# Moving the weight and attention-vector loads of a graph kernel out of its first phase

## The chip, the cores and the metric

One core of one Trainium2 chip. The metric is the device time of one execution in microseconds (us); the kernel before takes 2069.59 us, the median of 3 runs.

## The reference, cut to what matters

One block of two graph layers over 3750 nodes and 63750 edges that come sorted by destination, 256 features, 8 relations, 4 heads.

```
h = max(layernorm(x), 0)
feat = einsum('ni,rhid->rnhd', h, conv_weights)      # conv_weights: 8 x 4 x 256 x 64
el, er = sum(feat_src * attn_l[edge_type]), sum(feat_dst * attn_r[edge_type])
alpha = softmax over the edges of a destination of leaky_relu(el + er)
x = x + segment_sum(alpha * feat_src) + h_bias
h = max(layernorm(x), 0)
x = x + (linear layer, 3 rounds of mean over neighbours with two 256 x 256 products and relu, linear layer)(h)
```

## The kernel before

The kernel is a row of phases. Each phase is a `nc.Block()`: inside it every engine has its own list of instructions, ordered by semaphores, and at its end all engines meet before any goes on. So a phase lasts as long as its longest engine. DMAs are issued by SP or ACT, each on a queue of its own; an engine that issues a DMA is held while it does so, and the end of a block waits for the issue, not for the landing (the landing has a semaphore of its own, which the user of the data waits for).

The phases at the start, by the line of their block:

- **L327, loading.** SP loads the four integer lists (`dst` twice, `src`, `edge_type`) into `hT`, three DMAs for each list: 3 x 16384 entries, 114 rows of 128, and a rest of 6 (L332, L334, L336). ACT loads the attention vectors, spread to all 128 partitions, into `side` (L342, two DMAs of 1024 KB) and then the weights into `wbuf` (L346, sixteen DMAs of 128 KB, in rows of 256 bytes). POOL makes iotas and fills pads. DVE converts the lists to f32 (L385) when all of them have landed.
- **L396, `tile_ends()`.** DVE picks the first and last key of each tile of 128 edges, PE turns them into a row, DVE copies the row out of PSUM (L400 to L405). ACT, SP and POOL have nothing to do. The function is called a second time with a flag, inside `sort_edges`, for lists that do not come sorted.
- **L424, checks.** DVE works out with a chain of small instructions whether the lists are sorted and spread as planned (L428 to L452); PE has one matmul.
- **L489 and following.** The sort, which is jumped over here, the tile tables (L625), the windows and the load of `x` (L740), then the layer norm and the attention columns (L889). In the last one DVE and POOL multiply the weights by the attention vectors (L914, L932), after a wait for all 18 transfers on the semaphore `s_at` (`s_at` is used nowhere else).
- Behind them the feature tables and the adjacency table (L1133 on, from about 155 us), the walk over the edges, and three aggregation rounds that PE fills.

Of the kernel before, what the change touches and what calls it, by code (L numbers as in the profile page):

```python
# [34 lines left out]
P = 128  # L35
N, E, F, R, H, D = 3750, 63750, 256, 8, 4, 64
LAYERS = 3
K2 = F // P
# [61 lines left out]
def gnn_kernel(nc, x, src, dst, etype, conv_w, attn_l, attn_r, h_bias, w_in, b_in, w_agg, w_self,  # L100
               b_hid, w_out, b_out, out):
    ctx = ExitStack()
    with ctx:
# [15 lines left out]
        def sem(name):  # L119
            names[name] = names.get(name, 0) + 1  # L120
            s = nc.alloc_semaphore(f"{name}_{names[name]}")
            phase_sems.append(s)
            return s
# [157 lines left out]
        def when(eng, flag):  # L281

            if flag is None:
                return nullcontext()
            return eng.If(eng.value_load(flags_i[0:1, flag:flag + 1], min_val=0, max_val=1) > 0)
# [20 lines left out]
        wc = wbuf[:, :].rearrange("p (k n) -> p k n", k=K2)  # L306
        x_all = work[:, 0:8192].rearrange("p (b f) -> p b f", b=32)

        s_ld, s_xl, s_at = [nc.alloc_semaphore(a) for a in ("vectors_loaded", "all_x_loaded", "weights_in")]
# [15 lines left out]
        attn = [side[:, 2048 * i:2048 * (i + 1)] for i in range(2)]  # L325

        with nc.Block() as block:  # L327
            @block.sync
            def _(sp):
                sp.wait_ge(s_pad, 4)  # L330
                for a, buf in zip((dst, dst, src, etype), raw):
                    sp.dma_start(buf[:, 0:3, :], a[0:3 * P * P].rearrange("(c p j) -> p c j", c=3, p=P)  # L332
                                 ).then_inc(s_rl, 16)
                    sp.dma_start(buf[0:whole, 3, :], a[3 * P * P:E - rest].rearrange("(p j) -> p j", j=P)  # L334
                                 ).then_inc(s_rl, 16)
                    sp.dma_start(buf[whole:whole + 1, 3, 0:rest],  # L336
                                 a[E - rest:E].rearrange("(o j) -> o j", o=1)).then_inc(s_rl, 16)

            @block.scalar
            def _(act):  # L340
                for a, buf in zip((attn_l, attn_r), attn):
                    act.dma_start(buf, a.rearrange("(o r) h d -> o (r h d)", o=1).to_broadcast([P, 2048])  # L342
                                  ).then_inc(s_at, 16)
                for k in range(K2):
                    for r in range(R):
                        act.dma_start(wc[:, k, r * F:(r + 1) * F].rearrange("p (h d) -> p h d", h=H),  # L346
                                      conv_w[r, :, k * P:(k + 1) * P, :].rearrange("h p d -> p h d")
                                      ).then_inc(s_at, 16)

            @block.gpsimd  # L350
            def _(pool):
                pool.iota(io_i[:, 0:P], pattern=[[1, P]], base=0, channel_multiplier=0).then_inc(s_io, 1)
                pool.iota(io_i[:, P:P + 1], pattern=[[1, 1]], base=0, channel_multiplier=1).then_inc(s_io, 1)
                pool.iota(lists_i[:, 0:CQ], pattern=[[1, CQ]], base=0, channel_multiplier=0).then_inc(s_io, 1)
                pool.iota(lists_i[:, CQ:], pattern=[[P, NTW]], base=0, channel_multiplier=0).then_inc(s_io, 1)
                for a, v in zip((key, dstm, srcr, typr), (N - 1, -1, PADSRC, 0)):
                    pool.memset(a[:, CR:CT, :], float(v)).then_inc(s_tail, 1)
                pool.memset(fidx_i[:, CR * P:T + U], 0).then_inc(s_tail, 1)
                pool.memset(col_t[:, CR * P:T], -1.0).then_inc(s_tail, 1)
                pool.memset(code_t[:, CR * P:T], 0.0).then_inc(s_tail, 1)  # L360
                pool.memset(typ_t[:, CR * P:T], 0.0).then_inc(s_tail, 1)
                pool.memset(dstloc[:, CR * P:T], -1.0).then_inc(s_tail, 1)
                at = 0
                for c, end in enumerate(CHUNK_END):
                    pool.memset(thr[0:1, at:end + 1], float(c * CW)).then_inc(s_tail, 1)
                    at = end + 1
                pool.wait_ge(s_tail, 9 + NC)

            @block.vector
            def _(dve):  # L370
                for v, buf in zip((N - 1, -1, PADSRC, 0), raw):
                    dve.memset(buf[:, 3:CR, :], v).then_inc(s_pad, 1)
                dve.memset(ones[:, :], 1.0)
                dve.memset(eps_c[:, :], EPS)
                c = Chain(dve, s_c)
                dve.wait_ge(s_io, 2)
                c.link(dve.tensor_copy(iota_w[:, :], io_i[:, 0:P]))
                c.link(dve.tensor_copy(iota_p[:, :], io_i[:, P:P + 1]))
                c.link(dve.tensor_scalar(ident[:, :], iota_w[:, :], iota_p[:, :], None, ALU.is_equal))
                dve.wait_ge(s_io, 4)  # L380
                c.link(dve.tensor_copy(iota_c[:, :], lists_i[:, 0:CQ]))
                c.link(dve.tensor_copy(win_f[:, :], lists_i[:, CQ:]))
                dve.wait_ge(s_rl, 48 * 4)
                for buf, to in zip(raw, (key, dstm, srcr, typr)):
                    dve.tensor_copy(to[:, 0:CR, :], buf[:, 0:CR, :]).then_inc(s_cv, 1)  # L385
                dve.wait_ge(s_cv, 4)
# [3 lines left out]
        base_r, last_r = stg[0:1, 0:T], stg[0:1, T:2 * T]  # L390
        first_c, last_c = small[:, 36:36 + CT], small[:, 44:44 + CT]

        def tile_ends(flag=None):

            s_fc, s_tp, s_br = sem("ends_picked"), sem("ends_turned"), sem("ends_rowed")
            with nc.Block() as block:  # L396
                @block.vector
                def _(dve):
                    with when(dve, flag):
                        dve.tensor_copy(first_c, key[:, :, 0]).then_inc(s_fc, 1)  # L400
                        dve.tensor_copy(last_c, key[:, :, P - 1]).then_inc(s_fc, 1)
                        dve.wait_ge(s_tp, 1)
                        for i, to in enumerate((base_r, last_r)):
                            dve.tensor_copy(to[:, 0:512], PS[0:1, 2 * i, :]).then_inc(s_br, 1)
                            dve.tensor_copy(to[:, 512:T], PS[0:1, 2 * i + 1, 0:T - 512]).then_inc(s_br, 1)  # L405
                        dve.wait_ge(s_br, 4)
                        dve.sem_inc(passed, 1)

                @block.tensor
                def _(pe):  # L410
                    with when(pe, flag):
                        pe.wait_ge(s_fc, 2)
                        for i, c1 in enumerate((first_c, last_c)):
                            for c in range(CT):
                                mm = pe.transpose(PS[0:1, 2 * i + c // 4, (c % 4) * P:(c % 4 + 1) * P],
                                                  c1[:, c:c + 1], ident[:, :])
                        mm.then_inc(s_tp, 1)

        tile_ends()


        s_k, s_ks = sem("check_steps"), sem("check_sum")
        bad, viol = small[:, 0:4], stg[:, 2048:2048 + CR * (P - 1)].rearrange("p (c j) -> p c j", c=CR)
        with nc.Block() as block:  # L424
# [29 lines left out]
            @block.tensor  # L454
            def _(pe):
                pe.wait_ge(s_k, 2)
                pe.matmul(PS[0:1, 0, 0:1], bad[:, 0:1], ones[:, 0:1], start=True, stop=True).then_inc(s_ks, 1)

# [9 lines left out]
        def sort_edges(flag, key_array, other_array):  # L470
# [127 lines left out]


            tile_ends(flag)  # L600

        end_phase()
# [1687 lines left out]
```

## Time and profile before

| | |
|---|---|
| runs | 2069.22, 2069.59, 2075.5 us |
| profiled execution | 2072.4 us, of which the span from first to last instruction is 2070.6 us |
| mean granted TensorE clock | 0.901 |
| busy | PE 1778.8 us (86%), ACT 1143.4 (55%), DVE 1081.7 (52%), POOL 521.1 (25%) |
| first phase (L327) | 0 to 19.0 us |
| tile ends (L396) | 19.0 to 25.1 us |
| checks (L424) | 25.1 to 31.7 us, the end of DVE's last instruction in it |

An engine's busy time does not count the issuing of DMAs: ACT is shown as idle in the first phase although its queue instructions fill it. The queue of an engine has a name of its own in the views, SPq or ACTq.

### The profile page before, as it was taken

The numbers are of one execution on the slowest core, as the hardware profiler recorded it, in microseconds if no ns is written. First come the engines' busy times: TensorE is split into PE (matmuls) and PEld (weight loads), VectorE is DVE, ScalarE is ACT, GpSimd is POOL, SyncE is SP. The second block draws the span as 40 slices with busy tenths as digits, with TensorE's granted clock in tenths as the row PEclk, the third lists the DMA queues.
The fourth block names the chain that finished last, engine by engine and source line by source line (L and its number), as shares of the span: only waits on it lengthen the run. The fifth ranks groups of instructions, "written<-read, shape, count | busy, mean of one in ns | idle before, by whom it ended". The sixth has DMA issues, their size and how long they took to land. (4 is left out here: it accounts for less than half of the span.)

```text
span 2070.6 us, 26209 instructions
## 1 busy us (share of the span) xinstructions
PE 1778.8 (86%) x7604; PEld 1236.5 (60%) x7605; DVE 1081.7 (52%) x3126; ACT 1143.4 (55%) x2498; POOL 521.1 (25%) x544
## 2 busy tenths in 40 slices
PE   1159999999497879798797955999989999999998
PEld 1054444444375557565575634777777777877777
DVE  4858888888365676766767535453550000301011
ACT  0034455565387779797787734454545444544442
POOL 2600000000577777777777300000000000000000
PEclk7569999999687789797898887999999999999999
DMA  4314555555655566565665325333324333363432
GB/s 129 82 14 152 171 195 192 181 201 199 202 146 161 152 182 176 153 188 159 171 173 161 101 63 181 99 123 107 110 77 128 113 116 112 98 208 123 135 123 62
DMA packets 285221, 290.67 MB, mean 140 GB/s; under 512 B 88673, under 2 KB 248102, under 8 KB 284806
## 3 DMA queue, kind: packets, MB, share of 16 engines
q1 hardware_dynamic: 235094, 186.23, 29.3%
q0 software_dynamic: 23952, 66.46, 12.1%
q10 hardware_dynamic: 26016, 36.15, 4.8%
q8 instruction: 64, 1.05, 0.2%
q14 instruction: 95, 0.78, 0.1%
HBM read 201.26 MB, written 87.48 MB: 139 GB/s over the span
## 5 line engine op out<-in xcount | busy, mean ns | idle before, releaser
L1141 POOL DMA_INDIRECT work<-feat_tab,fidx_i x499 | 477.6, 957 | 586.0 <-issue 581.2
L2117 PE MATMUL PS<-a_pe,y_hi 128*128 128x512 f32 (+2 forms) x1440 | 556.7, 392 | 33.4 <-ACT a_pe L2014 33.4
L2117 PE MATMUL PS<-a_pe,y_lo 128*128 128x512 f32 (+2 forms) x1440 | 536.7, 379 | 0.0
L2014 ACT ACTIVATE a_pe<-a_in 128x1536 fp32r<-128x1536 f16 (+1 forms) x240 | 329.3, 1376 | 342.7 <-PE PS L2117 329.1
L2117 PEld LDWEIGHTS PS<-a_pe,y_hi 128*128 128x128 f32 (+1 forms) x1440 | 274.0, 190 | 103.1 <-ACT a_pe L2014 35.0
L1210 ACT ACTIVATE work<-work 128x64 f32<-128x64 f32 x1344 | 325.1, 332 | 0.0
L2117 PEld LDWEIGHTS PS<-a_pe,y_lo 128*128 128x128 f32 (+1 forms) x1440 | 274.2, 190 | 55.2 <-issue 6.7
L1385 PE MATMUL PS<-work,stg 128*128 128x260 f32 x1008 | 289.6, 437 | 6.5 <-ACT work L1210 4.6
L1385 PEld LDWEIGHTS PS<-work,stg 128*128 128x128 f32 x1008 | 207.5, 217 | 65.0 <-issue 19.6
L255 DVE TENSOR_SCALAR side<-iota_c,work 128x512 f16<-128x512 f16 x705 | 245.8, 349 | 0.0
L1325 PE MATMUL PS<-wbuf,hT 128*128 128x512 f32 x480 | 226.9, 595 | 0.0
L2221 DVE TENSOR_TENSOR mean<-PS,rdeg 128x1024 f32<-128x1024 f32 (+1 forms) x24 | 27.2, 1135 | 363.3 <-PE PS L2117 363.0
L273 ACT ACTIVATE side<-PS 128x512 f16<-128x512 f32 x235 | 128.7, 595 | 142.0 <-PE PS L265 69.6
L254 DVE TENSOR_SCALAR side<-iota_c,rel 128x128 f16<-128x128 f16 x705 | 176.9, 251 | 49.1 <-PE PS L265 48.3
L265 PE MATMUL PS<-side 128*128 128x512 f16 x705 | 173.6, 381 | 24.6 <-DVE side L255 16.1
L265 PEld LDWEIGHTS PS<-side 128*128 128x128 f16 x705 | 68.3, 98 | 151.2 <-DVE side L255 36.1
L1335 PE MATMUL PS<-er_win,stg 128*128 128x32 f32 x1008 | 134.9, 294 | 22.5 <-ACT stg L1196 22.5
L1335 PEld LDWEIGHTS PS<-er_win,stg 128*128 128x128 f32 x1008 | 129.9, 211 | 26.4 <-ACT stg L1196 24.5
L1325 PEld LDWEIGHTS PS<-wbuf,hT 128*128 128x128 f32 x480 | 91.8, 191 | 75.1 <-issue 57.9
L1181 ACT ACTIVATE stg<-PS 128x512 f32<-128x512 f32 x120 | 72.0, 600 | 43.3 <-PE PS L1325 42.5
L1588 DVE TENSOR_TENSOR work<-work,PS 128x1024 f32<-128x1024 f32 x42 | 51.3, 1221 | 69.1 <-ACT work L1202 69.1
L1579 DVE TENSOR_TENSOR stg<-PS,dstloc 128x512 f32<-128x512 f32 x126 | 86.4, 686 | 1.5
(257 smaller groups left out, 1674.0 us busy)
## 6 DMA issues: line engine op xcount, KB each, us to landing
a_in<-a_tab SPq DMA_DIRECT2D x210, 384.0 KB, 3.2
feat_tab<-stg ACTq DMA_DIRECT2D x120, 260.0 KB, 2.2
a_tab<-side SPq DMA_DIRECT2D x235, 128.0 KB, 1.8
stg<-dst_tab SPq DMA_DIRECT2D x42, 384.0 KB, 4.0
work<-feat_tab,fidx_i POOLq DMA_INDIRECT x499
h_tab<-outs SPq DMA_DIRECT2D x42, 130.0 KB, 2.6
h_tab<-outs SPq DMA_DIRECT2D x8, 520.0 KB, 3.9
stg<-h_tab SPq DMA_DIRECT2D x8, 520.0 KB, 4.1
```

The source lines that it names most:

```text
L254: dve.tensor_scalar(code[:, s, :], iota_c[:, 0:P], rel[:, k, j:j + 1], None, ALU.is_equal)
L255: dve.tensor_scalar(other[:, s, :], iota_c[:, :], pairs_in[:, w, j, 1:2], None, ALU.is_equal).then_inc(built.pair, 1)
L265: pe.matmul(PS[:, BBS[w % len(BBS)], :], code[:, s, :], other[:, s, :], start=(j == 0), stop=(j == DEPTH - 1)).then_inc(built.free, 1)
L273: act.activation(counts[:, w % KEPT_W, :], PS[:, BBS[w % len(BBS)], :], ACT.Copy).then_inc(built.evicted, 1)
L1141: pool.indirect_dma_start(out=ring[:, s, 0:FE], out_offset=None, in_=feat_tab[:, :], in_offset=bass.IndirectOffsetOnAxis(ap=idx, axis=0)). ...
L1210: ins = act.activation(a, a, ACT.Copy, scale=ring[:, s, F + h:F + h + 1])
L1325: mm = pe.matmul(PS[:, cc, :], hT[:, k, b * P:(b + 1) * P], wc[:, k, cc * 512:(cc + 1) * 512], start=(k == 0), stop=(k == K2 - 1))
L1335: mm = pe.matmul(PS[:, ERB, u * RH:(u + 1) * RH], onehotT[:, u * P:(u + 1) * P], er_win[:, :], start=True, stop=True)
L1385: mm = pe.matmul(PS[:, OUTS[j], 0:EXT], onehot[:, t, :], ring[:, j * U + t, 0:EXT], start=(t == 0), stop=(t == U - 1), skip_group_check=True)
L1579: dve.tensor_tensor(onehot[:, q * QT:(q + 1) * QT, :], IOTA_PS.unsqueeze(1).to_broadcast([P, QT, P]), dstloc[:, tiles_of(i, j, q, QT)].uns ...
L2014: act.activation(a_pe[:, load % A_PE, :, 0:n], a_in[:, load % A_IN, :, 0:n], ACT.Copy).then_inc(s_conv, 1)
L2117: mm = pe.matmul(SUMS(ug, n)[:, f, :], y[0:rows_of, kb, f * P:(f + 1) * P], a_pe[0:rows_of, load % A_PE, kb % KB, 0:n], start=(kb == 0 and ...
```

## The change

The last lines of the diff below stand in the block of the checks (L424). The sixteen weight loads leave the first phase. They are issued in the first call of `tile_ends()`, eight by ACT (the first half of the input features, k = 0) and eight by SP (k = 1). The two loads of the attention vectors are issued by ACT in the phase of checks. In the first phase ACT has nothing left. The semaphore, its count and its waits stay as they are.

```
             @block.scalar
-            def _(act):
-                for a, buf in zip((attn_l, attn_r), attn):
-                    act.dma_start(buf, a.rearrange("(o r) h d -> o (r h d)", o=1).to_broadcast([P, 2048])
-                                  ).then_inc(s_at, 16)
-                for k in range(K2):
-                    for r in range(R):
-                        act.dma_start(wc[:, k, r * F:(r + 1) * F].rearrange("p (h d) -> p h d", h=H),
-                                      conv_w[r, :, k * P:(k + 1) * P, :].rearrange("h p d -> p h d")
-                                      ).then_inc(s_at, 16)
-
...
+        def load_weights(eng, k):
+            for r in range(R):
+                eng.dma_start(wc[:, k, r * F:(r + 1) * F].rearrange("p (h d) -> p h d", h=H),
+                              conv_w[r, :, k * P:(k + 1) * P, :].rearrange("h p d -> p h d")).then_inc(s_at, 16)
+
+        def load_attention(eng):
+            for a, buf in zip((attn_l, attn_r), attn):
+                eng.dma_start(buf, a.rearrange("(o r) h d -> o (r h d)", o=1).to_broadcast([P, 2048])).then_inc(s_at, 16)
+
         def tile_ends(flag=None):
...
             with nc.Block() as block:
+                if flag is None:
+                    @block.scalar
+                    def _(act):
+                        load_weights(act, 0)
+
+                    @block.sync
+                    def _(sp):
+                        load_weights(sp, 1)
...
+            @block.scalar
+            def _(act):
+                load_attention(act)
```

The instructions of ACT from the start of the program to the tile tables, of the kernel before (`UNCONDITIONAL_BRANCH` rows enter and leave a phase):

```order
L2280 ISA
L339 UNCONDITIONAL_BRANCH
L342 DMA side<-in_L_gnn_attn_l 128x2048
L342 DMA side<-in_L_gnn_attn_r 128x2048
L346 DMA wbuf<-in_L_gnn_conv_weights 128x4x64 x16
L327 UNCONDITIONAL_BRANCH
L713 UNCONDITIONAL_BRANCH
```

And of the changed kernel, the same stretch:

```order
L2291 ISA
L396 UNCONDITIONAL_BRANCH
L384 DMA wbuf<-in_L_gnn_conv_weights 128x4x64 x8
L394 UNCONDITIONAL_BRANCH
L466 UNCONDITIONAL_BRANCH
L389 DMA side<-in_L_gnn_attn_l 128x2048
L389 DMA side<-in_L_gnn_attn_r 128x2048
L431 UNCONDITIONAL_BRANCH
```

The loads are split over two phases, weights first, and eight of the weight loads are gone from ACT.

SP of the kernel before, from its last list to the sort:

```order
L332 DMA hT<-in_edge_type 128x3x128
L334 DMA hT<-in_edge_type 114x128
L336 DMA hT<-in_edge_type 1x6
L327 UNCONDITIONAL_BRANCH
L490 UNCONDITIONAL_BRANCH
```

And of the changed kernel, with eight weight loads between the first phase and the sort:

```order
L336 DMA hT<-in_edge_type 1x6
L327 UNCONDITIONAL_BRANCH
L400 UNCONDITIONAL_BRANCH
L384 DMA wbuf<-in_L_gnn_conv_weights 128x4x64 x8
L394 UNCONDITIONAL_BRANCH
L501 UNCONDITIONAL_BRANCH
```

SP's twelve loads of the lists keep their order and stand ahead of every weight load.

## Rows read from the trace of the kernel before

**Rows 1.** The page's chain that ended last, by engine: shares of the span.

```profile
PE 37%; DMA 1%; DVE 1%; ACT 0%; issue 0%; SPq 0%; ACTq 0%; DVEq 0%
```

**Rows 2.** Timeline from 0, DVE: start, duration, what [idle before, released by].

```profile
15.70 1.43 DVE L385 CAST hT<-hT 128x512 f32<-128x512 int32 x4 [12.14 <-DMA hT<-in_edge_type]
19.02 0.17 DVE L400 COPY small<-hT 128x7 f32<-128x7 f32 x1 [1.89 <-PEq L327]
...
24.17 0.53 DVE L405 COPY stg<-PS 1x384 f32<-1x384 f32 x1
25.14 0.69 DVE L428 TENSOR_TENSOR stg<-hT 128x508 f32<-128x508 f32 x1 [0.43 <-PEq L396]
...
31.53 0.14 DVE L452 TENSOR_SCALAR flags_i<-small 1x1 int32<-1x1 f32 x1
```

**Rows 3.** Timeline from 0, queue instructions of ACT: start, duration.

```profile
0.74 0.39 ACTq L342 DMA_DIRECT2D side<-in_L_gnn_attn_l  x1
1.16 0.45 ACTq L342 DMA_DIRECT2D side<-in_L_gnn_attn_r  x1
1.64 16.92 ACTq L346 DMA_DIRECT2D wbuf<-in_L_gnn_conv_weights  x16
```

**Rows 4.** Timeline from 0, queue instructions of SP.

```profile
1.45 0.46 SPq L332 DMA_DIRECT2D hT<-in_dst  x1
1.96 0.41 SPq L334 DMA_DIRECT2D hT<-in_dst  x1
...
3.41 0.61 SPq L334 DMA_DIRECT2D hT<-in_dst  x1
4.06 1.10 SPq L336 DMA_DIRECT2D hT<-in_dst  x1
...
6.18 1.80 SPq L336 DMA_DIRECT2D hT<-in_src  x1
...
8.99 1.01 SPq L336 DMA_DIRECT2D hT<-in_edge_type  x1
```

**Rows 5.** DMA view, 0 to 20 us: busy tenths in 40 slices; queues: packets, MB, share.

```profile
DMA  0005999989897979999999999999999889999999
q10 hardware_dynamic: 8409, 4.12, 79.3%
q1 hardware_dynamic: 2088, 1.02, 21.7%
```

**Rows 6.** DMA view, 16 to 18 us: the queue of ACT (q10).

```profile
q10 hardware_dynamic: 1825, 0.45, 104.3%
```

**Rows 7.** DMA view, 18 to 22 us: ACT's queue and the weight loads' landing.

```profile
q10 hardware_dynamic: 2182, 0.54, 72.2%
wbuf<-in_L_gnn_conv_weights ACTq DMA_DIRECT2D x2, 128.0 KB, 3.2
```

**Rows 8.** Line L346: issue durations in ns, and landing.

```profile
L346 ACTq DMA_DIRECT2D wbuf<-in_L_gnn_conv_weights x16: 456/808/2867, 1.6 to 18.0; - x16
DMA to landing us min/median/max: 3.1/4.8/9.5
```

**Rows 9.** DMA view, 0 to 150 us: a small load: KB each, median us to landing.

```profile
work<-pair_tab SPq DMA_DIRECT2D x78, 3.0 KB, 1.6
```

**Rows 10.** Timeline, later stretches: the next transfer, and the users of the weights.

```profile
43.72 0.42 SPq L703 DMA_DIRECT2D mask_tab<-stg  x1
...
83.22 4.49 POOL L932 TENSOR_TENSOR stg<-wbuf,side 128x2048 f32<-128x2048 f32 x1 [10.26 <-POOLq L740]
83.23 6.63 DVE L914 TENSOR_TENSOR stg<-wbuf,side 128x2048 f32<-128x2048 f32 x1 [3.25 <-PEq L740]
```

**Rows 11.** Stretches: us, busy of PE, PEld, DVE, ACT, POOL, PEclk, DMA share, GB/s.

```profile
200.00:400.00 200.00, 191.75 (x631) 84.24 (x630) 168.14 (x766) 104.82 (x250) 0.00 (x0) 1.00 0.56 182
600.00:1200.00 600.00, 511.39 (x2419) 366.98 (x2418) 402.23 (x1126) 474.00 (x1539) 426.77 (x446) 0.83 0.57 160
```

More of the change, by code:

```diff
@@ L337, in _ @@
                                  a[E - rest:E].rearrange("(o j) -> o j", o=1)).then_inc(s_rl, 16)
-            @block.scalar
-            def _(act):
-                for a, buf in zip((attn_l, attn_r), attn):
-                    act.dma_start(buf, a.rearrange("(o r) h d -> o (r h d)", o=1).to_broadcast([P, 2048])
-                                  ).then_inc(s_at, 16)
-                for k in range(K2):
-                    for r in range(R):
-                        act.dma_start(wc[:, k, r * F:(r + 1) * F].rearrange("p (h d) -> p h d", h=H),
-                                      conv_w[r, :, k * P:(k + 1) * P, :].rearrange("h p d -> p h d")
-                                      ).then_inc(s_at, 16)
             @block.gpsimd
```

## The prediction

> **What bounds the kernel now.** I read the page's chain first. It holds only the end: PE fills the aggregation rounds, and the start of the program doesn't appear in it [rows 1]. The change touches nothing there, so the question is only when the later work begins. Since all engines meet at the end of each phase, a phase that ends earlier by some microseconds should move all that follows by as much. I therefore read the timeline of the first phases, engine by engine, for what each phase ends with.
>
> In the first phase DVE waits until 15.70 us for the last of the integer lists and then converts for 1.43 us, to 17.13 [rows 2]. ACT is later still: its sixteen weight issues fill 1.64 to 18.56 [rows 3]. DVE goes on at 19.02, released by the end of the phase. So ACT's issuing ends the phase, and DVE's wait for the lists stands 1.43 us behind it.
>
> Why the lists are late is in the queue instructions and the DMA view. SP's first issues follow each other by (3.41 - 1.45) / 4 = 0.49 us, but from 4.06 on some of them take 1.01 to 1.80 us [rows 4]. All DMA engines are nearly always busy from 1.5 us to 20 us, and of the 5.14 MB that they move 4.12 MB are ACT's (q10) and only 1.02 MB the lists (q1) [rows 5]. The lists share the engines with transfers that nobody needs before 83 us [rows 10].
>
> **The first phase without ACT's loads.** SP keeps its twelve issues. At 0.49 us each the last begins at 1.45 + 11 x 0.49 = 6.84 us. When has it landed? The nearest small load, from SP and onto idle engines, lands 1.6 us after its issue [rows 9], which gives 8.4. A weight load with others of its queue ahead of it lands after 3.1 at best [rows 8], which gives 9.9. The lists' packets took 21.7% of 16 engines over 20 us for 2088 packets, or 33 ns each, beside the others [rows 5]; spread evenly that is 130 x 33 ns = 4.3 us per engine, less than the 5.4 us over which the issues are spread, so little can pile up. I take 8.8 us, near the lower end.
>
> The Trainium skill has a rule that is a little less kind (DMA: Bandwidth & Descriptors, "Why a DMA increments its semaphore by 16 and not by 1"): a transfer runs on the largest number of engines up to 16 that divides its slowest dimension. By it the 114-row loads use six engines only, and these have 24 + 19 packets per list, 172 in all, which at 33 ns is 5.7 us; begun at about 2.5 us, one us behind the first issue, they end at 8.2 and the wake-up comes some 0.6 us later. By the even spread and the lower bound the landing would be at 8.4 and the next phase 8.7 us earlier; by this rule the landing can't be before 8.8, and it is 8.3. No row here shows which engine takes which packet.
>
> Behind the landing DVE's 1.43 us of conversions stay, and from DVE's last instruction of a phase to its first of the next it is 25.14 - 24.70 = 0.44 us [rows 2]. The next phase then begins at 8.8 + 1.43 + 0.44 = 10.7 us in place of 19.02: **8.3 us earlier**. The bounds, 8.4 and 9.9 for the landing, make it 8.7 and 7.2.
>
> **The phase of the tile ends with sixteen weight issues in it.** DVE and PE need 24.70 - 19.02 = 5.7 us there [rows 2], and ACT and SP have been idle; that is the cover. A weight issue into a queue with room costs 0.46 us at least [rows 8], and with the gap between two issues (1.16 - 0.74 - 0.39 = 0.03 [rows 3]) eight would take about 4 us: hidden. What can spoil it is that the queues fill. 16.92 / 16 = 1.06 us was the mean issue when the engines were full [rows 3], and eight of those are 8.5 us, 2.8 us more than the cover. So the bounds are 0 and 2.8 us.
>
> Which is nearer depends on how many loads a queue takes before it holds its engine. The engines move weights at 0.45 MB in 2 us [rows 6], so one load of 0.131 MB each 0.58 us. From 18.0 us on 0.54 MB are still to be moved [rows 7]; by the end of the last issue at 18.56 some 0.13 MB of these have gone, and 0.41 MB, three loads, are in the queue, without that issue having been slow. With three loads in each of the two queues, ten must have been drained when the last issue is through: 10 x 0.58 us and one us until the first packet (0.74 to some 1.8 in [rows 3, 5]) are 6.8 us, 1.1 more than the cover. With four in each queue it is 8 x 0.58 + 1 = 5.6 us, and nothing shows. I estimate four, as ACT's first issues went in next to two 1 MB loads, and put **0.3 us** of loss.
>
> **The phase of the checks.** ACT's two issues of attention vectors took 0.39 and 0.45 us [rows 3]. They may have to wait for the weights to drain: sixteen loads are through 1 + 16 x 0.58 = 10.3 us after the tile ends began, some 4.3 us into the checks. DVE's chain lasts 31.67 - 25.14 = 6.5 us, so they are covered with 2 us to spare; if that cover were gone, a load of 1024 KB would hold the phase for its own issue only, under a microsecond. DVE and PE of this phase touch neither tile.
>
> **Who waits for the moved loads.** Weights are through at 10.7 + 10.3 = 21 us. The attention vectors are 2 MB in large packets; ACT's queue moved its 4.12 MB in about 19 us beside all else, so 2 MB are through in less than 9.5 us, at 30 us at the latest. The next other transfer is issued at 43.72 - 8 = 36 us, and the users start at 83.2 - 8 = 75 us [rows 10]. Moving the loads costs their users nothing, with 45 us in hand.
>
> **The sum.** -8.3 + 0.3 + 0 = -8.0 us. The profiled execution took 2072.4 us, so its like would take 2064.4; it is 2.8 us above the median of the runs. Against the median: 2069.6 - 8.0 = **2061.6 us**. That is 0.39%; 0.3%, about what a measurement of this kernel can tell from no change, is 6.2 us.
>
> **Rivals.**
>
> - *The queues fill in the tile-ends phase, and ACT or SP ends it.* For it: in the trace nearly all of ACT's weight issues are above the 0.46 us of the shortest (median 0.81, longest 2.87 [rows 8]), and both queues now push at once into engines that drain one load in 0.58 us. Against it: the queues start empty. It costs up to 2.8 us: a gain of 5.5, 2064.1 us, within 0.3%. Two us of it decide. Chance 14%.
> - *The lists are slow by themselves.* For it: the slow issues are always the third of a list, the load of 6 entries, and no row shows that issue without ACT's traffic but the first. If the three slow ones (1.10, 1.80, 1.01 [rows 4]) stay so, the last issue begins at 8.99 as before and lands at 10.6, 1.8 us behind my 8.8: a gain of 6.2, 2063.4 us. Chance 8%.
> - *Slower, by TensorE's clock.* From 200 to 400 us the granted clock is 1.00, the full 2.4 GHz; from 600 to 1200 us the mean is 0.83, so for a third of it, about 204 us, it is at 1.2 GHz, with PE busy 511 of 600 us [rows 11]. PE's work there is cut by waits for gathered rows, and the level changes with them. A shifted start could let more of it fall on the low level. A microsecond at the low level costs half a microsecond at most; to turn 8 us gained into 6.2 lost needs 14.2 us, or 28 us more at the low level, 232 in place of 204. The runs of before differ by 6.3 us with nothing changed, less than half of that. Chance 4%, at 2076 us. The Trainium skill (TensorE: Matmul & The Clock Gate, Part 1) says that the monitor behind this clock runs freely and isn't reset when the kernel starts; by it a shift of 8 us draws new places for the changes but no more of them, which no run so far shows.
> - *The gain is given back, or the loads' place does nothing.* It would take a wait on something that doesn't move with the phases. I found none: every later DMA is issued behind the end of a phase. The same clock can eat 3 to 6 us, though. Chance 9%, 2064 to 2069 us.
>
> **How the numbers follow.** The forecast has 65%: 2060.3 to 2063 us from the bounds of the landing (8.7 and 7.2) and a loss of 0 to 1.1, with some tenths for the clock. The low end of the range is 2059.6. Upwards it takes in the filling queues and the slow lists and part of the give-back, to 2066.5. Faster by over 0.3% (below 2063.4): the forecast but for a small part, and half of the slow lists: 0.66. Within 0.3%: filling queues, the rest of the slow lists, the give-back: 0.30. Slower: 0.04.
>
> **What would show it.** In the profile after: the conversions of the lists begin between 8.4 and 9.9 us; no queue instruction of SP in the first phase is longer than 0.6 us; the first copy of the tile ends at about 10.7 us and the first check at about 17.1, when the last issue of ACT and SP is through; the first checks have two attention issues beside them that end before them; the product of weights and attention vectors begins at 75.2 us and waits for no DMA. I am wrong if the first phase ends later than 12.5 us, if the tile-ends phase lasts over 8 us, or if the 8 us are there at 75 us and gone at the end, which the mean clock of the later stretches would show.

## The result and the profile after

| | before | changed |
|---|---|---|
| median | 2070.32 us (9 runs, 2063.84 to 2078.3) | 2061.33 us (9 runs, 2056.71 to 2071.22) |
| profiled execution, span | 2072.4, 2070.6 us | 2056.7, 2054.9 us |
| mean granted TensorE clock | 0.901 | 0.916 |

The ratio is 0.9955, 95% interval 0.9934 to 0.9975: 0.45% faster, 9 us between the medians. 2061.6 us and 8.0 us had been forecast. (The kernel before has nine runs here, three of them those of the table ahead.)

The timeline of the changed kernel's start, DVE and the two queues (start, duration, what [idle before, released by]), answering to [rows 2 to 4]:

```profile
1.45 0.46 SPq L332 DMA_DIRECT2D hT<-in_dst  x1
...
3.58 0.28 SPq L336 DMA_DIRECT2D hT<-in_dst  x1
...
5.93 0.28 SPq L336 DMA_DIRECT2D hT<-in_edge_type  x1
...
8.93 1.43 DVE L374 CAST hT<-hT 128x512 f32<-128x512 int32 x4 [5.37 <-DMA hT<-in_edge_type]
10.86 5.37 SPq L384 DMA_DIRECT2D wbuf<-in_L_gnn_conv_weights  x8
10.86 5.89 ACTq L384 DMA_DIRECT2D wbuf<-in_L_gnn_conv_weights  x8
10.89 0.17 DVE L407 COPY small<-hT 128x7 f32<-128x7 f32 x1 [0.53 <-PEq L327]
...
16.05 0.53 DVE L412 COPY stg<-PS 1x384 f32<-1x384 f32 x1
17.18 0.55 ACTq L389 DMA_DIRECT2D side<-in_L_gnn_attn_l  x1
17.22 0.69 DVE L435 TENSOR_TENSOR stg<-hT 128x508 f32<-128x508 f32 x1 [0.64 <-PEq L394]
17.75 0.49 ACTq L389 DMA_DIRECT2D side<-in_L_gnn_attn_r  x1
...
23.62 0.14 DVE L459 TENSOR_SCALAR flags_i<-small 1x1 int32<-1x1 f32 x1
28.44 0.69 DVE L641 SCALAR_TENSOR_TENSOR hT<-hT 128x512 f32<-128x512 f32 x1 [4.68 <-PEq L394]
```

The reader is to see four things. The conversions begin at 8.93 in place of 15.70 us, and they, no longer ACT, end the first phase: the first copy of the tile ends stands at 10.89 in place of 19.02, 8.1 us earlier. In the tile ends ACT is through with its issues at 10.86 + 5.89 = 16.75 us, a little behind DVE's last copy at 16.58, and the idle time at the end of the phase has grown from 0.43 to 0.64 us: the cover of 5.7 us was too short by 0.2 us. The attention issues end at 18.2, far inside the checks. And the first instruction of the tile tables stands at 28.44 us, where it stood at 36.36: 7.9 us of shift.

The product of weights and attention vectors, answering to [rows 10]:

```profile
74.89 4.49 POOL L943 TENSOR_TENSOR stg<-wbuf,side 128x2048 f32<-128x2048 f32 x1 [9.84 <-POOLq L751]
74.91 6.63 DVE L925 TENSOR_TENSOR stg<-wbuf,side 128x2048 f32<-128x2048 f32 x1 [2.83 <-PEq L751]
```

83.23 - 74.91 = 8.3 us, and it is the end of a phase that releases both, no DMA. (0.4 us of the 8.3 arise between the tile tables and the product. This stretch takes 46.9 us in the three profiles with the loads in the first phase and 46.4 to 47.0 in the others, so these 0.4 us are within its scatter.) The last packet of the weights ends at 21.8 us and that of the attention vectors at 27.9, where 21 and "30 at the latest" had been forecast. The moved loads cost their users nothing.

The two profiled executions differ by 2070.6 - 2054.9 = 15.7 us, twice that. The last matmul of the feature table (L1325, now L1336) begins at 527.8 us before and 519.5 after, still 8.3 us apart; the last one of the walk over the edges (L1385, now L1396) at 1201.3 and 1185.1, 16.2 us apart:

```profile
L1336 PE MATMUL PS<-wbuf,hT x480: 592/592/1057, 151.9 to 519.5; 128*128 128x512 f32 x160
```

```profile
L1396 PE MATMUL PS<-work,stg x1008: 382/383/800, 565.8 to 1185.1; 128*128 128x260 f32 x168
```

(min/median/max of the duration in ns, first and last start in us.) So this pair gained another 7.9 us inside the walk. There the granted clock was 0.85 in place of 0.83 [rows 11]:

```profile
600.00:1200.00 600.00, 502.61 (x2408) 358.47 (x2407) 410.05 (x1137) 471.95 (x1530) 419.91 (x439) 0.85 0.56 160
```

Over the nine runs of the changed kernel the clock and the time go together: 0.916 has 2056.71 us and 0.898 has 2071.22, with a correlation of -0.78. The spread between executions is 14.5 us wide here, and the profiled execution happens to be the fastest of the nine, so I count these 7.9 us as spread. That the clock causes them isn't shown: in the 27 runs of the kernel before beside e5 to e8 it has a correlation of -0.07 with the time. Nor does the clock explain the gain: its mean is 0.907 over those 27 runs and 0.904 to 0.907 over the runs of each of e5 to e8, which are 9 to 11 us faster.

### The profile page after: what moved, and what is told of

Read it like the earlier page. It is cut to its first block and busy times, and to the rows that moved or that the text cites. A ratio compares the mean times of both kernels' runs of the same rounds, so it can differ in the third digit from the quotient of the medians.

```text
span 2054.9 us, 26209 instructions
## 1 busy us (share of the span) xinstructions
PE 1770.4 (86%) x7604; PEld 1230.3 (60%) x7605; DVE 1081.3 (53%) x3126; ACT 1143.4 (56%) x2498; POOL 520.6 (25%) x544
## 3 DMA queue, kind: packets, MB, share of 16 engines
q8 instruction: 64, 1.05, 0.2%
## 5 line engine op out<-in xcount | busy, mean ns | idle before, releaser
L1396 PE MATMUL PS<-work,stg 128*128 128x260 f32 x1008 | 288.3, 435 | 8.0 <-ACT work L1221 6.2
L1396 PEld LDWEIGHTS PS<-work,stg 128*128 128x128 f32 x1008 | 205.6, 215 | 65.7 <-issue 16.0
L1336 PE MATMUL PS<-wbuf,hT 128*128 128x512 f32 x480 | 226.1, 593 | 0.0
L1336 PEld LDWEIGHTS PS<-wbuf,hT 128*128 128x128 f32 x480 | 91.6, 191 | 74.9 <-issue 57.7
```

Of the source, the lines that this page charges most:

```text
L1336: mm = pe.matmul(PS[:, cc, :], hT[:, k, b * P:(b + 1) * P], wc[:, k, cc * 512:(cc + 1) * 512], start=(k == 0), stop=(k == K2 - 1))
L1396: mm = pe.matmul(PS[:, OUTS[j], 0:EXT], onehot[:, t, :], ring[:, j * U + t, 0:EXT], start=(t == 0), stop=(t == U - 1), skip_group_check=True)
```

## The experiments

Twelve runs, ten of them new kernels and two of them repeats (e8, e12). The early marks are the measure: in each profile the start of the conversions, of the first copy of the tile ends, of the first check, and of the product of weights and vectors. The ratio is to the kernel before, run on the same chip in between. It goes by all the runs of both and isn't the quotient of the two medians beside it. e9 and e10 leave out edges, ran once and have no ratio.

| kernel | conversions | first copy | first check | product | kernel before, this (median us) | ratio (95%) |
|---|---|---|---|---|---|---|
| before | 15.70 | 19.02 | 25.14 | 83.2 | | |
| changed | 8.93 | 10.89 | 17.22 | 74.9 | 2070.32, 2061.33 | 0.9955 (0.9934 to 0.9975) |
| e1_act_waits | 8.97 | 23.04 | 29.16 | 87.2 | 2277.98, 2281.86 | 1.0023 (1.0010 to 1.0035) |
| e2_attention_stays | 12.36 | 14.32 | 20.80 | 78.6 | 2277.98, 2271.47 | 0.9961 (0.9945 to 0.9976) |
| e3_one_queue | 9.03 | 10.99 | 20.23 | 78.3 | 2277.98, 2269.31 | 0.9969 (0.9953 to 0.9986) |
| e4_start_put_back | 19.16 | 21.12 | 27.24 | 84.7 | 2277.98, 2276.08 | 0.9991 (0.9977 to 1.0005) |
| e5_lists_two_queues | 8.49 | 10.45 | 16.88 | 75.0 | 2074.84, 2064.49 | 0.9958 (0.9937 to 0.9978) |
| e6_lists_all_engines | 8.62 | 10.59 | 17.18 | 75.3 | 2074.84, 2065.57 | 0.9947 (0.9926 to 0.9967) |
| e7_weights_in_checks | 8.85 | 10.81 | 16.93 | 75.5 | 2074.84, 2064.98 | 0.9939 (0.9921 to 0.9957) |
| e8_change_again | 9.20 | 11.16 | 17.42 | 75.1 | 2074.84, 2064.18 | 0.9946 (0.9925 to 0.9967) |
| e9_even_lists_only | 8.11 | 10.07 | 16.62 | | | |
| e10_uneven_lists | 8.19 | 10.15 | 16.76 | | | |
| e11_single_loads_last | 8.58 | 10.54 | 16.98 | 75.2 | 2073.20, 2064.56 | 0.9962 (0.9942 to 0.9983) |
| e12_before_again | 16.14 | 19.25 | 25.37 | 83.5 | 2257.31, 2255.16 | 0.9998 (0.9984 to 1.0013) |

In two of the groups, e1 to e4 and e12, every kernel took about 200 us more, all of it in the walk over the edges (in e12, the kernel before itself, its last matmul begins at 1379.5 us and not at 1201.3; the last of the feature table at 527.3 and not at 527.8). They are compared only with the kernel before beside them. The chip isn't the reason: e1 to e4 and e5 to e8 ran on the same one, beside a kernel before of 2278 and of 2075 us.

**e1: the kernel before, ACT waits for the lists.**

```
             def _(act):
+                act.wait_ge(s_rl, 48 * 4)
                 for a, buf in zip((attn_l, attn_r), attn):
```

> The kernel before, with one wait added: ACT begins its eighteen loads in the first phase only when all lists have landed. It tells the two halves of the gain apart, the lists' contention and ACT's issuing. My theory: both are needed, since ACT's issues alone end the phase. The lists then land at about 8.9 us as in the changed kernel, the conversions begin there, but ACT issues from 8.9 on: 2 x 0.45 + 16 x 0.56 = 9.9 us, and the first copy of the tile ends begins at about 19.2 us, as in the kernel before (19.02). Median within 2 us of the kernel before. Rival, the lists' contention is all that counts: the first copy at about 11 us, and 8 us faster.

The conversions begin at 8.97 us as in the changed kernel, and nothing is won: the first copy begins at 23.04, 4.0 us later than before. ACT's queue:

```profile
8.90 0.39 ACTq L343 DMA_DIRECT2D side<-in_L_gnn_attn_l  x1
9.33 0.45 ACTq L343 DMA_DIRECT2D side<-in_L_gnn_attn_r  x1
9.80 12.78 ACTq L347 DMA_DIRECT2D wbuf<-in_L_gnn_conv_weights  x16
```

The theory holds and its size was off: the sixteen issues take 12.78 us, 0.80 each, not 0.56, and the median is 3.9 us above the kernel before, not within 2. The excess is in the third to the fifth weight issue (1.40, 0.99 and 2.64 us): ACT is held there while the attention vectors move, whose last packet ends at 15.8 us. From then on an issue takes 0.53 to 0.56 us again, but for the last (0.72). Both halves are needed: loads that leave the lists alone gain nothing as long as ACT issues them in the same phase.

**e2: the attention vectors stay in the first phase.** The block of the checks loses its two loads, and the first phase gets them back:

```
+            @block.scalar
+            def _(act):
+                for a, buf in zip((attn_l, attn_r), attn):
+                    act.dma_start(buf, a.rearrange("(o r) h d -> o (r h d)", o=1).to_broadcast([P, 2048])
+                                  ).then_inc(s_at, 16)
```

> The changed kernel, with the two attention loads (2 MB, large packets) left to ACT in the first phase. My theory, the engines of the DMA are shared between the queues: the lists (1 MB) wait for part of the 2 MB, which take about 6 us alone; they land at 10 to 12 us in place of 8.9, and the first copy of the tile ends begins at 12 to 14 us: a gain of 5 to 7 us over the kernel before in place of 8. Rival, only the weights with their small packets held the lists up: conversions at 8.9 us as in the changed kernel, first copy at 10.9.

Two megabytes in large packets beside the lists cost them 3.4 us (12.36 in place of 8.93). The theory holds, with sizes a little over its ranges: 12.36 where 10 to 12 was expected, a first copy at 14.32 where it was 12 to 14, and 4.7 us gained at the product in place of 5 to 7. Two of SP's issues show the hold as in the kernel before; these rows and the next two blocks are timelines of SP and DVE:

```profile
3.61 1.39 SPq L336 DMA_DIRECT2D hT<-in_dst  x1
...
5.91 1.85 SPq L336 DMA_DIRECT2D hT<-in_src  x1
```

The weights with their small packets and the attention vectors each take a share of the 6.8 us that the lists were late; about half is the attention vectors'.

**e3: all sixteen weight loads on ACT.**

```
                         load_weights(act, 0)
-
-                    @block.sync
-                    def _(sp):
-                        load_weights(sp, 1)
+                        load_weights(act, 1)
```

> The changed kernel, with all sixteen weight loads on ACT in the phase of the tile ends, none on SP. My theory: sixteen issues at 0.56 us are 8.9 us or more, so ACT ends the phase at 10.9 + 9 = 19.8 and the first check begins at about 20.2 us in place of 17.2: 3 us slower than the changed kernel, 5 us faster than before. Rival, the engines drain at the same pace whatever the queue and the queue holds most of it: first check at 17.2 to 17.5 us, no difference from the changed kernel.

```profile
16.15 0.54 DVE L409 COPY stg<-PS 1x384 f32<-1x384 f32 x1
20.23 0.69 DVE L432 TENSOR_TENSOR stg<-hT 128x508 f32<-128x508 f32 x1 [3.55 <-PEq L394]
```

DVE has done its part at 16.69 and stands idle for 3.55 us until ACT is through: sixteen issues in 8.81 us, 0.55 each. That is the forecast of this experiment to the tenth, and what the split over two engines saves: 3 us. The Trainium skill (DMA: Bandwidth & Descriptors, "Issuing engines are not separate DMA queues") says that issuing from several engines saves only the sequencer's time for the issue, "usually small relative to the DMA itself". The trace agrees on what is saved: the last packet of the weights ends at 21.85 us with one queue and at 21.76 with two. But here, where a phase ends with the issues and not with the landings, the issue time is all that counts.

None of the sixteen issues is longer than 0.53 us: the engines drain a load in about 0.6 us, as the prediction had it, and one queue alone doesn't fill. With two queues it does. The DMA view of the changed kernel from 10.8 to 16.75 us, where ACT's eighth issue ends:

```profile
q1 hardware_dynamic: 2302, 0.57, 50.8%
q10 hardware_dynamic: 2107, 0.52, 48.0%
```

ACT has issued eight loads (1.05 MB) and 0.52 MB have been moved: four loads stand in its queue. ACT's first long issue (0.79 us, at 13.60) and SP's (1.05 us, at 14.04) begin with five and six loads issued and 1.2 and 2.1 moved, so with about four in the queue as well.

**e4: the start put back.**

```
                 dve.wait_ge(s_rl, 48 * 4)
+                for _ in range(11):
+                    c.link(dve.memset(work[:, 0:768], 0.0))
```

> The changed kernel, with eleven clears of an unused stretch of memory (about 0.75 us each, 8.2 us together) on DVE behind the wait for the lists, so that the first phase ends at about 19 us again while all loads stay where the change put them. My theory, the whole gain is the earlier start: time of the kernel before, 2070 us, within 3 us. Rival, a part of the gain comes from elsewhere (the 15.7 us between the two profiled executions against 8.3 us at the start): it stays faster than before, at 2062 to 2065 us.

The clears took 0.93 us each with the wait between them, so the first copy begins at 21.12 and the product at 84.7 us, 1.4 us later than in the kernel before. The gain is gone: 0.9991, an interval that holds 1. It is the earlier start that makes the change faster. By the marks it should have been 1.4 us slower, and its median is 1.9 us lower; more on that below.

**e5: the lists on two queues.** ACT is idle in the first phase; it takes two of the four lists.

```
+            @block.sync
+            def _(sp):
+                load_lists(sp, ((dst, raw[0]), (dst, raw[1])))
+
+            @block.scalar
+            def _(act):
+                load_lists(act, ((src, raw[2]), (etype, raw[3])))
```

> The changed kernel, with the lists issued half by SP (dst twice) and half by ACT (src, edge types), which is idle in the first phase. Last issue then at about 3.9 us in place of 5.9. The question is what the lists' landing at 8.9 hangs on, since in the changed kernel it comes 3.0 us behind the last issue and not 1.6 to 2 as I had it. Theory A, the 114-row loads run on six DMA engines only, and these have 172 packets each: the issues don't matter, conversions begin at 8.5 to 9.0 us as before, and the time is that of the changed kernel. Theory B, the landing follows the last issue by 3 us: conversions at about 6.9, 2 us faster than the changed kernel.

```profile
3.81 0.31 ACTq L335 DMA_DIRECT2D hT<-in_edge_type  x1
...
8.49 1.43 DVE L381 CAST hT<-hT 128x512 f32<-128x512 int32 x4 [4.93 <-DMA hT<-in_edge_type]
```

The last issue begins at 3.81 us in place of 5.93, and the conversions move from 8.93 to 8.49 only (8.85 to 9.20 in the five profiles with this first phase and all lists on SP). The lists' landing hangs little on when the last one is issued. Theory B falls; theory A is left, but no more than that. The DMA view of the changed kernel, 2 to 10 us (tenths of 16 engines, 40 slices of 0.2 us), shows its engines partly idle, with a tail of four tenths and less from 7.0 us on; the last packet ends at 8.55:

```profile
DMA  0004599543768547799746697444332100000000
```

**e6: 112 and 2 rows.**

```
+                    for p0, p1 in ((0, 112), (112, whole)):
+                        eng.dma_start(buf[p0:p1, 3, :], a[3 * P * P + p0 * P:3 * P * P + p1 * P].rearrange(
+                            "(p j) -> p j", j=P)).then_inc(s_rl, 16)
```

> As the kernel before it in this row (lists half on SP, half on ACT), and the 114 rows of each list split into 112 and 2, so that one more DMA is issued for each list but the 112 rows can spread evenly. Theory A (six engines carry the 114-row loads): the packets now spread to 130 for each engine in place of 172 on six, 3.6 to 4.3 us from 2.5 on; conversions begin at 6.5 to 7.5 us, and the first copy of the tile ends at 8.4 to 9.4 in place of 10.9: 1.5 to 2.4 us faster than the changed kernel. Theory B (issues and a fixed tail of 3 us): last issue at about 4.5, conversions at 7.5, no better than half a us against the kernel without the split, which would itself be at 6.9.

The conversions begin at 8.62 us, no better than in e5. Theory A had put them at 6.5 to 7.5 and theory B at 7.5: neither holds as it stood. The same DMA view of e6 shows a pause at about 5 us that e5 hasn't, and packets that end at 7.3 us, 1.3 us before the conversions:

```profile
DMA  0004455999998501457999996300000000000000
```

So two more questions were open: does the row count matter at all, and what do the short loads do?

**e9 and e10: two DMAs for each list, 112 or 114 rows.**

```
-                    eng.dma_start(buf[whole:whole + 1, 3, 0:rest],
-                                  a[E - rest:E].rearrange("(o j) -> o j", o=1)).then_inc(s_rl, 16)
```

and in e9 `buf[0:112, 3, :]` in place of `buf[0:whole, 3, :]`.

> Lists half on SP, half on ACT, with two DMAs for each list only: 3 x 16384 entries and 112 rows of 128. It leaves out the last 262 edges, so the rest of the program works on other data and only the first 20 us are read. Eight DMAs, all with rows that spread evenly: 129 packets of 27 ns for each engine are 3.5 us from 2.4 on. If the short loads and uneven rows make the landing late (the kernel with 16 DMAs had a pause of 0.6 us in the middle and woke DVE 1.2 us after its last packets), conversions begin at 6.4 to 6.8 us. If the lists' megabyte is limited by the memory or by all DMA engines together, they begin at 8 us or later.

> As the one before, with 114 rows in place of 112; it leaves out the last 6 edges, and only the first 20 us are read. If the 114 rows are carried by six DMA engines, these have 172 packets of 27 ns, 4.6 us from 2.4 on: conversions begin at 7.4 to 7.9 us, about 1 us later than with 112 rows, and the busy share of the DMA view falls to four tenths and below for its last microsecond. If the row count doesn't matter, they begin when the 112 rows do, within 0.2 us.

The same view of e9:

```profile
DMA  0002525999999999999997511000000000000000
q1 hardware_dynamic: 1056, 0.51, 22.9%
```

And of e10:

```profile
DMA  0003566899999999997544444431000000000000
q1 hardware_dynamic: 1040, 0.51, 24.1%
```

With 112 rows the engines are all busy until about 6.2 us and done a microsecond later. With 114 rows the share falls to four tenths at about 6.0 us and stays there for more than a microsecond: six of sixteen engines are 0.375. The rule of the Trainium skill that the prediction weighed (DMA: Bandwidth & Descriptors, "Why a DMA increments its semaphore by 16 and not by 1": the largest number of engines up to 16 that divides the slowest dimension) is borne out by the shape of this tail. The packets of q1, which has two lists, fit it too: a list has 1056 / 2 = 528 in e9 for its 496 rows and 1040 / 2 = 520 in e10 for its 498, so 32 and 22 more than rows, which would be one for each engine of a load (16 + 16 and 16 + 6).

And yet DVE wakes at 8.11 us in e9 and 8.19 in e10, where 6.4 to 6.8 (or 8 and later) and 7.4 to 7.9 had been forecast. With even rows it wakes 1.0 us behind the end of the packets (7.1 us), with uneven rows 0.6 us behind it (7.6 us). The trace records each update of the semaphore that DVE waits for. In e9 sixteen of its 128 updates come after the last packet, the last at 8.01 us; in e10 the last comes at 8.09. So in e9 it is the updates that are late, not the data; why they are, no run shows. With the lists on two queues the tail of six engines is real and its removal gains 0.1 us, less than the marks repeat; on one queue, as in the changed kernel, it wasn't tried. Leaving out the short loads (e10 against e5, e9 against e6) is worth 0.3 and 0.5 us, each from one profile.

**e11: the 6-entry loads last.** Each queue issues its two large loads, its two of 114 rows, then its two of 6 entries (three loops over `lists` in place of one).

> The whole computation: lists half on SP, half on ACT as in e5, with the loads ordered by size: both large ones of a queue, both of 114 rows, and the two of 6 entries last. If the 6-entry loads in the middle hold up what is queued behind them, the conversions begin at 7.5 to 8 us (e5: 8.49); if only the sum on the six engines counts, at 8.3 to 8.6. Against the changed kernel at most 1 us, too little for the median to tell.

8.58 us, as e5 (8.49): the order of the short loads doesn't matter.

**e7: the weights in the checks.** The two blocks leave `tile_ends()`; the block of the checks has

```
             def _(act):
+                load_weights(act, 0)
                 load_attention(act)
+
+            @block.sync
+            def _(sp):
+                load_weights(sp, 1)
```

> The changed kernel, with the sixteen weight loads one phase later, in the phase of the checks (eight by ACT, then its two attention loads, and eight by SP). It tells how well each phase covers the issues. Eight issues took ACT 5.89 us in the tile ends, 0.17 us longer than DVE's chain, and the phase began to end 0.2 us late. In the checks the cover is 6.5 us, and ACT needs 5.9 + 1.0 for the two attention loads: about 0.3 us more than the cover. So the tile ends phase 0.2 us shorter, the checks 0.3 longer: no difference from the changed kernel (within 0.5 us at the tile tables, 28.4 us). Rival, the attention issues stall behind full queues of weights (up to 2.8 us each in the trace of before): tile tables begin at 30 to 32 us.

```profile
16.90 5.89 ACTq L384 DMA_DIRECT2D wbuf<-in_L_gnn_conv_weights  x8
22.82 1.12 ACTq L389 DMA_DIRECT2D side<-in_L_gnn_attn_l  x1
23.97 0.46 ACTq L389 DMA_DIRECT2D side<-in_L_gnn_attn_r  x1
```

DVE's last check instruction ends at 23.48, ACT at 24.43. The tile ends are 0.2 us shorter (6.12 from first copy to first check, in place of 6.33), the checks 0.9 us longer where 0.3 had been forecast, and the tile tables begin at 29.05 us, 0.6 us later than in the changed kernel and just outside the 0.5 of the forecast. The issue of the first attention load takes 1.12 us behind the weights; the stall of the rival is there, in small. The product stands at 75.5. The place that the change chose is the better one by 0.6 us, too little for the medians.

**e8: the changed kernel again.**

> The changed kernel again, beside the others on their chip, as the one to compare with; the chip of the experiments so far took 2278 us for the kernel before where the first took 2070. If the gain is a shift of the start, it is the same 8 us here: 2270 us beside 2278, ratio 0.9965, and the marks at the start as in the first profile (conversions 8.9, first copy 10.9, first check 17.2, tile tables 28.4). If it hung on TensorE's clock in the walk over the edges, it would be different on this chip, anything from 0 to 16 us.

Marks as the first time within 0.3 us, a shift of 83.2 - 75.1 = 8.1 us, and 0.9946. The first result repeats. The kernel before took 2075 us beside it and not 2278, so it doesn't tell whether the gain is the same when the walk is slow.

**e12: the kernel before again.**

> The kernel before, against itself. The kernels with the loads moved measure 0 to 5 us faster than their earlier start explains: 1 us for the change itself, 4.3, 2.0 and 3.4 for the second to fourth experiment, 0.5, 3.1, 5.0 and 3.1 for the next four, 0 for the last, and the first one, which keeps the loads in the first phase, 1.2 slower. If this excess is the spread of the comparison, the kernel before measures itself at 1.000 with an interval of 0.002 about it, and single comparisons of the same kernel may be 0.1 to 0.2% off either way. If the excess belongs to the moved loads, this one is within 0.05% of 1.000.

0.9998, but with an interval 0.0029 wide, and medians 2.15 us apart between two kernels that are the same. By the marks set ahead, a value within 0.05% of 1 speaks for an excess that belongs to the moved loads; but it also lies where the other reading wanted it, so one such comparison doesn't decide.

## Why the prediction was right, point by point

- **What ends the first phase** (ACT's issues, with the lists' wait 1.4 us behind): right. e1 shows it from the other side: lists early and ACT late gain nothing.
- **The next phase begins at 10.7 us:** 10.89. The value is right and its working is not. I put the last issue at 6.84 and its landing 2 us later. The last issue begins at 5.93, since the 6-entry loads take 0.28 us to issue when ACT's loads are away, and the conversions begin 3.0 us later. The two errors cancel, which is luck. The step that failed is "so little can pile up": the last packet of the lists ends at 8.55 us, 2.3 us behind the last issue, and in e5, with all issues through by 4.1 us, the conversions move by 0.4 only. What sets the landing comes behind the issues: the transfer and, in e6 and e9, semaphore updates up to 1.2 us behind the last packet. The prediction's other sum, by six engines, had the last packet at 8.2 us and the landing at 8.8. It is the nearer one (8.55 packets, 8.84 the last update), but since even rows gained only 0.1 us in e9, it isn't shown to be the cause.
- **0.3 us lost in the tile ends:** 0.2. With room in the queue an issue takes 0.39 to 0.53 us; the last two of SP and the last three of ACT take more, up to 1.2. They begin to be held when four loads stand in the queue, which is the estimate that the prediction chose over three (1.1 us of loss): right in its mechanism. e3 gives the price without the split, 3.1 us.
- **Checks and users of the loads at no cost:** right (18.2 against 23.8 us; 74.9 us with no DMA waited for). e7 shows that the cover would not have held with the weights there: 0.6 us lost.
- **Every later phase moves by the same:** right to the end of the feature table, 8.3 us, as far as single profiles tell (see below). e4 puts the start back and the gain is gone.
- **Rivals.** Filling queues: there, at 0.2 us where 2.8 was its price. Slow lists by themselves: not so, the third issues of each list are short when ACT is away. TensorE's clock: it did not make the change slower; the profiled pair differs by 7.9 us in the walk, in the changed kernel's favour and with a higher granted clock (0.85 and 0.83), but that one causes the other isn't shown. That the loads' place does nothing: refuted.

**What stays open.** The moved loads measure somewhat more than the shift of the product explains: in us, worked out from the ratios (from the medians it is 0.6 to 3.8, and 0.1 for e1), 1.0 for the change, 3.1 on repeating it, 4.3, 2.0 and 3.4 for e2 to e4, 0.5, 3.1 and 5.0 for e5 to e7, 0 for e11, and the other way by 1.2 for e1. Most single ones are inside their intervals (e2, e4 and e7 are not quite), those of a group share one set of runs of the kernel before, and the kernel before misses itself by 2.15 us in its medians, by 0.0002 in its ratio. Whether 2 us of real gain beyond the start are in it, these runs can't tell, and single profiles scatter too much to find its place. From the product to the last matmul of the feature table it is 444.5 us before, 444.6 in the changed kernel, 441.8 in e4 (which makes up its late start there) and 449.5 in e6. From there to the last matmul of the walk it is 673.6 us before, and 665.6 to 674.2 in the six whole kernels with moved loads beside it; when the walk is slow it is 872.9 in e1, with the loads in the first phase, and 873.9 to 879.5 in e2 to e4.

## What to carry to other kernels

A load that nobody needs soon still costs twice when it is issued in the first phase: it takes DMA engines from the loads that are waited for, and it holds the phase's end for as long as its engine issues. Both have to be undone together (e1 undoes the first alone and gains nothing), and a phase whose queue engines are idle is the place for it, if the issues fit under the work there: count the issues per engine (here 0.55 us each), and split them over SP and ACT when they don't. The split stops helping where the queues fill, here at four loads in each. When a gain is below the spread of the executions, read it from the marks at the start of the phases, which repeat within 0.3 us in the changed kernel and within 0.5 in the kernel before, and let the median only confirm it.

## What the runs showed of the hardware that was not expected

- In the changed kernel a DMA of six entries in one row takes 0.24 to 0.28 us to issue, one of 114 or 128 rows 0.38 to 0.41 behind the first (0.46). On SP it is always the short one that is held for 1.0 to 1.9 us when ACT's loads are beside it (kernel before, e2).
- Sixteen weight issues take 8.81 us on an otherwise empty ACT queue (e3), and 12.78 us right behind two loads of 1024 KB (e1).
- An engine that issues loads of 128 KB in rows of 256 bytes begins to be held when four of them stand in its queue (changed kernel; the engines drain one in about 0.6 us).
- The semaphore of the lists is complete 0.3 us behind the last packet in the changed kernel, 0.5 in e10, 0.9 in e9 and 1.2 in e6, for the same megabyte.
- The same kernel took 2070 to 2075 or 2257 to 2278 us in different groups of runs, on one and the same chip too, with the whole difference in the walk over the edges (e12); the first 530 us were alike.
